# Decoder layer with routed experts: a turn of its own for the last attention chunk, and expert tiles planned from four chunks instead of five

## What is computed

```python
x = x + attn(_layernorm(x))                  # gated linear recurrence over time
x = x + xattn(_layernorm(x), ctx, ctx)       # 16 heads, 77 keys
x = x + ffn(_layernorm(x))                   # 4 experts, each token goes to 2

def ffn(xf):
    scores, idx = top_k(xf @ gate_W + gate_b, 2)
    weights = softmax(scores)
    expert(e) = layernorm(relu(layernorm(xf @ W1[e] + b1[e], g1[e], be1[e])) @ W2[e] + b2[e], g2[e], be2[e])
    return xf + sum over the two chosen experts of weight * expert(e)
```

## Time and profile before

| what | value |
|---|---|
| median of 3 runs | 1317.8 us |
| the profiled execution's own time | 1319.22 us |
| its span | 1317.5 us |
| PE busy | 1205.8 us (92%) |
| DVE busy | 943.1 us (72%) |
| ACT busy | 742.3 us (56%) |
| POOL busy | 435.3 us (33%) |
| chain that ended last | PE 68%, issue 9%, DVE 7%, DMA 5%, ACT 4%, POOL 3% |
| mean granted TensorE clock | 0.949 of full speed |

### The profile page before, as it was taken

One profiled execution on the slowest core, in us unless ns is written; L12 is line 12 of the kernel. 1 busy time (PEld: TensorE's weight loads), 2 busy tenths in 40 slices (PEclk: granted clock), 3 DMA queues, 4 the chain that ended last, 5 costly groups with the idle time before them and its releaser, 6 DMA issues.

```text
span 1317.5 us, 24951 instructions
## 1 busy us (share of the span) xinstructions
PE 1205.8 (92%) x6041; PEld 1004.9 (76%) x6042; DVE 943.1 (72%) x2197; ACT 742.3 (56%) x2119; POOL 435.3 (33%) x392
## 2 busy tenths in 40 slices
PE   5699999999679999999999979689999999999993
PEld 4478888888558888887888867567888888887882
DVE  6688888887635757777678776477777777777772
ACT  4333332233257766577666752276777777777772
POOL 1000000000023313445254434146655545454542
PEclk9789999999879989899899988799999999999996
DMA  9535443343420112022120239754444444444442
GB/s 299 175 128 194 141 158 136 122 156 133 154 82 1 41 57 97 9 93 77 56 96 9 89 119 322 238 161 68 81 80 79 80 79 80 79 80 78 80 66 39
DMA packets 78780, 142.09 MB, mean 108 GB/s; under 512 B 22810, under 2 KB 27086, under 8 KB 76917
## 3 DMA queue, kind: packets, MB, share of 16 engines
q1 hardware_dynamic: 60517, 89.46, 20.6%
q0 software_dynamic: 17056, 35.21, 15.2%
q10 hardware_dynamic: 1152, 16.78, 3.7%
HBM read 77.78 MB, written 66.78 MB: 110 GB/s over the span
## 4 chain that ended last, share of the span: by engine, by line
PE 68%; issue 9%; DVE 7%; DMA 5%; ACT 4%; POOL 3%; SPq 1%; DVEq 1%; POOLq 0%; ACTq 0%
PE banks L960 18%; PE banks L631 18%; PE banks L694 6%; PE banks L814 5%; PE banks L824 5%; PE banks L783 4%; PE banks L800 3%; DMA rows<-slot_table 2%; PE banks L840 2%; ACT rows L1153 2%; DVE operands L1355 2%; PE banks L986 2%; ACT operands L1050 1%; PE banks L972 1%; POOL slot_table L2132 1%
## 5 line engine op out<-in xcount | busy, mean ns | idle before, releaser
L960 PE MATMUL banks<-operands 128*128 x1608 | 390.9, 399 | 29.0 <-ACT banks L1272 13.2
L960 PEld LDWEIGHTS banks<-operands 128*128 128x128 f32 x1608 | 301.4, 190 | 98.9 <-issue 38.6
L631 PE MATMUL banks<-operands 128*128 128x512 f32 (+2 forms) x1224 | 301.1, 404 | 15.4 <-DVE operands L1355 9.4
L631 PEld LDWEIGHTS banks<-operands 128*128 128x128 f32 (+1 forms) x1224 | 233.2, 198 | 65.0 <-DVE operands L1355 8.6
L1355 DVE TENSOR_TENSOR operands<-banks,operands 128x512 fp32r<-128x512 f32 (+3 forms) x328 | 218.4, 682 | 70.1 <-ACT operands L1050 62.8
L1050 ACT ACTIVATE operands<-banks 128x512 fp32r<-128x512 f32 (+3 forms) x328 | 191.4, 603 | 132.2 <-PE banks L814 52.0
L1153 ACT ACTIVATE rows<-banks,score_shift 128x77 f32<-128x77 f32 x512 | 160.4, 361 | 42.2 <-DVE score_shift L1563 40.6
L1050 ACT ACTIVATE operands<-rows 128x512 fp32r<-128x512 f32 (+2 forms) x73 | 54.6, 751 | 173.9 <-DVE rows L1434 135.6
L1284 ACT ACTIVATE banks<-banks,param_cols 128x128 f32<-128x128 f32 x268 | 98.9, 429 | 89.4 <-PE banks L986 89.4
L2119 POOL TENSOR_TENSOR rows<-rows,score_rec 128x1232 f32<-128x1232 f32 x32 | 72.0, 2250 | 170.2 <-DVE score_rec L1571 170.2
L1153 ACT ACTIVATION_READ_ACCUMULATOR rows<-banks,score_shift 128x1 f32 x512 | 124.3, 244 | 0.0
(11 more groups left out here) (174 smaller groups left out, 1668.4 us busy)
## 6 DMA issues: line engine op xcount, KB each, us to landing
expert_parts<-operands SPq DMA_DIRECT2D x32, 512.0 KB, 3.3
operands<-expert_parts ACTq DMA_DIRECT2D x8, 2048.0 KB, 15.1
rows<-in_x SPq DMA_DIRECT2D x8, 1024.0 KB, 5.4
rows<-in_L_ffn_W SPq DMA_DIRECT2D x32, 256.0 KB, 3.7
x_rows<-rows SPq DMA_DIRECT2D x8, 1024.0 KB, 4.4
rows<-x_rows SPq DMA_DIRECT2D x8, 1024.0 KB, 5.8
xf_rows<-rows SPq DMA_DIRECT2D x32, 256.0 KB, 3.2
out<-rows SPq DMA_DIRECT2D x32, 256.0 KB, 2.6
```

Source lines behind the costliest of these rows:

```text
L631: last = nc.tensor.matmul(dst, stationary(a, k), moving(b, k), start=(t == 0 and k == 0), stop=(t == len(terms) - 1 and k == n_k - 1))
L960: last = nc.tensor.matmul(dst, stationary[:, a, k, :], weights[:, bass.ds(e, 1), w, a2, k, :].rearrange("p e f -> p (e f)"), start=False, ...
```

## The change

- `EARLY_CH` falls from 5 to 4, so `EARLY` from 37 to 29; `FRONT` rises from 12 to 18. The early plan moves from DVE's turn 7 into its turn 6 (`planned=True`), the totals from turn 6 to turn 5.
- Every slot load raises one semaphore, with no wait between loads. POOL (for its first gathers), DVE (before its tiles) and ACT (in tile 1) wait for all 29 early loads; after tile 17 all four engines wait for all 67.
- All eight weight loads move to SP; from the second on, each is issued only when the one before has landed. The second waits for the last projection.
- Chunks 6 and 7 get their base rows in place (`base_in_place`), and SP stores them later.
- The last turn gets its own function on each engine; POOL's has both first gathers between `normalise(c, 2)` and `normalise(c, 3)`. Chunk 7's attention output has its own place, and all its projections stand behind the turn.
- In every turn the second `xf_to_features` moves behind `scores(c, 3, (0, 1))`, ACT's third probability piece comes before `exp_scores(c, 2, (3,))`, and DVE's before `invert_sums(c, 2)`.
- Stage C: `weigh`, `slots` and the plan parts move behind `rows_lo` in DVE's tile and spread over tiles 2 to 10; POOL's scatters go one by one over tiles 1 to 12; two waits on slots in each DVE tile and one in each ACT tile go.

The `last_turn` shown in the diff is POOL's; those of PE, ACT and DVE are told above.

```diff
-EARLY_CH = NCH - 3
+EARLY_CH = NCH - 4
 EARLY = 2 * EARLY_CH * TPC - (NE - 1)
-FRONT = 12
+FRONT = 18
...
             engine.wait_ge(plan_ready, 2)
+            engine.wait_ge(slots_in, 16 * NSLOT)
             with engine.Fori(FRONT // 2, (NSLOT - 5) // 2) as n:
...
-            def load_slots(n, u):
-                i = 2 * n + u
+            def load_slots(i):
                 row = sp.value_load(plan_row[0:1, bass.ds(i, 1)], min_val=0, max_val=NE * REG - P)
-                need(sp, slots_in[u], 16 * n)
                 sp.dma_start(tile_slots[:, bass.ds(i, 1), :].rearrange("p i w -> p (i w)"),
-                             slots_d[bass.ds(row, P), :]).then_inc(slots_in[u], 16)
+                             slots_d[bass.ds(row, P), :]).then_inc(slots_in, 16)
...
+            sp.wait_ge(split_out, 16 * 4 * NCH)
             sp.wait_ge(mm_done, mm_num(last - 1, "q3") + 1)
+            load_expert(0)
             load_rows(b1_rows, "L0_ffn_b1", b1_in)
+            sp.wait_ge(plan_ready, 1)
+            sp.wait_ge(scattered, 16 * 2 * TPC * EARLY_CH)
+            with sp.Fori(0, EARLY) as i:
+                load_slots(i)
             for j in range(2):
                 store_xf(last - 1, j)
+            expert_in(0)
...
+            for j in range(TPC):
+                store_base(last - 1, j, slot3(last - 1)[:, j, :])
...
+            sp.wait_ge(mm_done, mm_num(NCH, "o3") + 1)
+            load_expert(1)
             for j in range(TPC):
                 store_xf(last, j)
+            expert_in(1)
+            for s in range(2, 2 * NE):
+                load_expert(s)
                 expert_in(s)
...
             sp.wait_ge(plan_ready, 2)
             sp.wait_ge(scattered, 16 * 2 * (NT - TPC))
             sp.wait_ge(scattered_aside, 16 * 2 * TPC)
-            with sp.Fori(EARLY // 2, NSLOT // 2) as n:
-                load_slot_pair(n)
-            load_slots(NSLOT // 2, 0)
+            with sp.Fori(EARLY, NSLOT) as i:
+                load_slots(i)
...
+            def base_in_place(c, j):
+                act.wait_ge(base_scaled, 2 * c + j // 2 + 1)
+                act.wait_ge(xf_ready, 4 * c + j + 1)
+                nc.scalar.activation(slot3(c)[:, j, :], slot3(c)[:, j, :], ACT.Identity, scale=base_scale[:, j:j + 1],
+                                     bias=base_shift[:, j:j + 1]).then_inc(base_ready, 1)
...
                 if early == 0:
-                    act.wait_ge(mm_done, mm_num(NCH, "o3") + 1)
-                    for s in (5, 6, 7):
-                        load_expert(s)
+                    act.wait_ge(b_t_done, t_num(NCH, "xf3") + 1)
+                    for j in range(TPC):
+                        act.wait_ge(xf_out[j], 16 * NCH)
+                    act.dma_start(be2_rows, io["L0_ffn_be2"].rearrange("e f -> (e f)").partition_broadcast(P).rearrange(
+                        "p (e f) -> p e f", e=NE)).then_inc(be2_in, 16)
...
+            def last_turn(c):
+                normalise(c, 0)
+                scatter(c - 3, 0)
+                scatter(c - 3, 1)
+                normalise(c, 1)
+                ln3_pow(c - 1, 0)
+                scatter(c - 3, 2)
+                scatter(c - 3, 3)
+                normalise(c, 2)
+                for u in range(2):
+                    gather(0, u, own=True)
+                normalise(c, 3)
+                ln3_pow(c - 1, 1)
...
                 if own:
-                    need_alone(pool, slots_in[u], 16 * (n + 1), pool_passed)
+                    need_alone(pool, slots_in, 16 * EARLY, pool_passed)
...
-                if 3 <= early < 7:
-                    scatter(last - 1, early - 3, aside=1)
-                if 8 <= early < 12:
-                    scatter(last, early - 8)
+                if 1 <= early < 5:
+                    scatter(last - 1, 2 + (early - 1) // 2, aside=1, ks=((early - 1) % 2,))
+                if 5 <= early < 13:
+                    scatter(last, (early - 5) // 2, ks=((early - 5) % 2,))
```

More of the change, by code:

```diff
@@ L612, in _ @@
+            for s in range(2, 2 * NE):
+                load_expert(s)
+                expert_in(s)
+            for j in range(TPC):
+                store_base(last, j, slot3(last)[:, j, :])
+            for i in range(2):
+                sp.wait_ge(base_out[i], 16 * 2 * NCH)
+            for j in range(TPC):
+                sp.wait_ge(xf_out[j], 16 * NCH)
             sp.wait_ge(plan_ready, 2)
@@ L926, in b_turn @@
                     gate_scores(c, (2,))
-                if ahead:
-                    scores(c + 1, 1, (0, 1))
+                scores(c + 1, 1, (0, 1))
                 if back:
@@ L948, in _ @@
             b_turn(1, back2=False)
-            with pe.Fori(2, NCH - 2) as c:
+            with pe.Fori(2, EARLY_CH + 1) as c:
                 b_turn(c)
-            b_turn(NCH - 2, totals=True)
-            b_turn(NCH - 1, ahead=False)
+            b_turn(EARLY_CH + 1, totals=True)
+            for c in range(EARLY_CH + 2, NCH - 1):
+                b_turn(c)
             def expert_product(dst, e, w, stationary, ready=None):
@@ L1003, in c_tile @@
                 hidden_in(i, u)
-                if early == 0:
-                    for j in (2, 3):
-                        xf_to_features(last, tail, j)
                 if after >= 3:
@@ L1218, in b_turn @@
                 exp_scores(c, 3, (2,))
[L1219 to L1220 removed]
+                q_hi(c + 1, 1)
                 pT_hi_part(c, 2, (2,))
                 exp_scores(c, 3, (3,))
[L1223 to L1226 removed]
                 if back:
@@ L1835, in b_turn @@
                     ln3_pair(c - 1, 1)
-                if not ahead:
-                    plan_early(0)
                 max_scores(c, 2, 1)
@@ L1841, in b_turn @@
                 pT_lo_part(c, 1, (0, 1))
-                if not ahead:
-                    plan_early(1)
                 if back:
@@ L2025, in c_tile @@
                     rows_lo(i + 3, 1 - u)
+                if early == 2:
+                    weigh(NCH - 1)
+                if early == 3:
+                    slots(NCH - 1, None)
+                if 4 <= early < 9:
+                    plan_late(early - 4)
+                if 9 <= early < 11:
+                    pack_plan(early - 9)
             last, tail = NCH - 1, NCH
-            rows_lo(0, 0)
+            last_turn(last)
             for j in range(2):
@@ L2031, in _ @@
             ln3_pair(last, 0)
+            weigh(last - 1)
+            x2_rows(last, tail, 2)
+            for j in range(2):
+                ln3_apply(last, tail, j)
+            x2_rows(last, tail, 3)
+            ln3_pair(last, 1)
             read_positions(tail)
+            slots(last - 1, tail, aside=1)
+            for j in range(2, TPC):
+                ln3_apply(last, tail, j)
+            rows_lo(1, 1)
             statistics(0, 0, m1_bank[0], m1_done, c1_stat)
```

437 lines of the change are left out of this document (234 added, 203 removed).

## The result

The changed kernel takes 1347.8 us (median of 4 runs, 1346.4 to 1348.7) against 1317.7 us of the kernel before: a ratio of 1.022, with a 95% interval from 1.0189 to 1.025. **It is slower by 30 us, a little over twice the 14 that were forecast**, inside the range only by its last 0.2 us and on the side that had most of the chance. Its profiled execution took 1347.4 us; the span is 1345.5.

What follows compares the result with a forecast made beforehand. PE, busy 92% of the span, was taken as the bound, with slot loads through SP stopping it 28 us at tile 18. Summed, 990.5 - 975.2 - 1.5 = +13.8: 1333.0 profiled, 1332 us median, range 1293 to 1348.

Steps and rivals of the forecast that it cites:

- (a): Order inside turns 1 to 6: 6.5 of 8.4 us of PE's waits for DVE saved, between 3 and 8.4.
- (b): Early plan in turn 6: its small DVE steps delay lo parts PE waits for, costing 1 us (0 to 4).
- (c): Early slots: 29 loads 1.45 us apart; the wait for them puts the last head group at 795.9, before 793.05.
- "free" start: Last head group's start at about 778.6 in the better last-turn order, if it did not wait for the slots.
- (d): Last head group to tile 1: 46 us, before 62.1; tile 1 at 841.9, where it was 855.2.
- (e): Tiles 1 to 12: 2.5 us off 80.1 (between 0 and 6), with tile 12 at 919.5.
- (f): Late slots: 37 distances of 1.45 us, all slots there at 987.6; PE stops 28 us at tile 18.
- first rival: Slot-load loop issues faster without waits, about 0.45 us apart; late slots arrive before tile 18: 1280 us, chance 0.17.
- (g): The 49 tiles behind tile 18: as before, with two waits fewer on DVE, 1.5 us less.
- The fast loop: Slot-load loop without waits runs near the DMA's pace, about 0.45 us apart: 1280 us, chance 0.17.
- The pace of straight line: Rival for the slot loads: the loop runs at straight-line spacing, 1.13 us: 1311, about no change, chance 0.13.
- The third: Rival in tile 0: ACT waits for chunk 7's xf stores behind a weight load, 8 us added: 1340, chance 0.12.

Runs made afterwards that it cites:

- the experiment: Changed kernel with GpSimd's first two gathers behind the last normalise and the rows of tiles 0 and 1 brought in later: 1351.5 us, ratio 1.0232.
- the first profile: Profile of the changed kernel as first measured, with no further edit: 1347.8 us median, ratio 1.022 against the kernel before.
- two steps: Changed kernel with three weights earlier and be2 from SP, 1349.4 us; then also the last two weights issued by ScalarE in tiles 8 and 9, 1351.1 us.
- the second: Profile of the changed kernel measured once more, unedited, on the chip of the experiments: 1351.5 us, ratio 1.0238 against the kernel before.
- the kernel with the two edits: Changed kernel with 24 tiles written out in front instead of 18 and slot loads in straight line: 1306.2 us, ratio 0.9914 against the kernel before.

## Why the prediction was right in kind and wrong in size

**(a), (b) Order of the turns, early plan: near in sum, by errors that cancel.** The six waits of the earlier trace rows are gone from the list over 400 to 753 us; in their place PE waits 2.7 us once for DVE. But from the last `attend` of chunk 0 to that of chunk 5, five turns took 271.6 us before and 254.4 after, 17.2 less, where I had 6.5 for six turns. PE's waits for DVE in them were 7.1 us. The rest is the clock: in three of the five turns before, the mean granted clock is 0.94 (somewhere in each the lower level), and in the five turns after it is 1.00. One such turn before and its like after, columns as in the earlier trace rows:

```profile
483.50:538.40 54.90, 53.85 (x302) 47.33 (x302) 39.37 (x95) 36.02 (x157) 18.14 (x13) 0.94 0.17 59
...
484.00:534.70 50.70, 50.64 (x302) 44.55 (x301) 39.96 (x95) 35.76 (x157) 15.57 (x11) 1.00 0.19 64
```

Against this, turn 6 with the early plan in it took 55.4 us, 4.5 more than the turn before it, where I had 1 (0 to 4), and chunk 0 ended 4.7 us later than before, for a reason that was not looked for. In sum chunk 6's last `attend` ended at 743.0 instead of 752.3, 9.3 us earlier instead of 5.5. The first slot load started at 744.87 us, forecast 746.7.

**(c) Early slots: right.** Spacing 1.49 (1.45), POOL's copy at 788.5 (789), last head group at 794.9 (795.9); the first load was 1.8 us early, which hid the spacing's 28 x 0.04 = 1.1. The "free" start, 778.6, was met by the experiment too: 780.1, with a first load 2.4 us later than in the first profile. What I had not seen is that this stop was no loss to be recovered by itself: taking it away gave nothing, because the first weight's count on SP and POOL's queue come out of the same slot loop. Of the 0.77 us between two loads that I called the row's number going into a register, and set beside the floor of about 600 ns in the Trainium skill's table ("DMA: Bandwidth & Descriptors", latency and other measured facts), the register load itself takes 0.27 us in the profile. The rest is further steps and the gaps between them, so the two figures do not agree; the measured one decides.

**(d) Last head group to tile 1: 52.0 us, not 46.** Tile 1 began at 847.0 instead of 841.9. PE waited 2.2 us for a low part, and tile 0's 24 matmuls ran in part at half clock (0.50 from 838.7 to 843), 7.8 us instead of 5.7 in tile 1, though the forecast had half clock only behind the stop at 794.9. A wait of 1.2 us stands in front of tile 0, whose rstd stood behind four scatter issues on POOL. PE's timeline:

```profile
827.42 3.07 PE L999 MATMUL banks<-operands 128*128 x12 [2.24 <-DVE operands L1405]
...
838.72 7.81 PE L999 MATMUL banks<-operands 128*128 x24
...
848.10 5.71 PE L999 MATMUL banks<-operands 128*128 x24
```

Which of it could be had back was not settled.

**(e) Tiles 1 to 12: the term that failed.** The prediction took 2.5 us off 80.1, with a worst case of nothing gained. Measured were 88.1, 10.5 more than forecast and 8.0 more than before: the term had the wrong sign. I counted DVE's and POOL's instructions and left out the transfers: with weights read one by one, five loads of 2 MB, started from 844.9 to 882.9, are under way in these tiles. The kernel before issued its last three in tile 0, and they had landed at 866.6, when its first scatter-add was issued. Scatter-adds and gathers, which DVE, POOL and PE wait for, land late beside the weights: 9.0 us instead of 4.8 and 6.2 instead of 4.3, as shown above. Taking the weights out in two steps gave 89.5, 84.5, 82.6.

The other part is the place of the extras: behind `rows_lo` they stand in front of the next tile's statistics. With weights earlier, tiles 7 to 11 took 38.3 us with extras behind and 35.9 in front (with 24 tiles in front and straight line beside it), 2.5 us; without, nothing, since the landings took the place. Part of what makes that place dear is a register load: each tile written out begins by reading an expert's number into a register (`expert_at`, L376), and behind the extras, which run one after the other, nothing covers it. VectorE's idle time before the statistics that follow an extra part (total, times, longest), in the changed kernel and in the experiment with the extras in front:

```profile
DVE moe_stats L2020 <- DVE expert_first_tile L1785: 0.8, 1, 0.8
...
DVE moe_stats L2020 <- DVE expert_first_tile L1785: 0.2, 1, 0.2
```

Over the nine places it is 7.8 us against 1.8. Neither part shows alone in the total. The 2.5 us that I took off never came: no experiment has less than 82.0 in these tiles, and the kernel before has 80.1.

The Trainium skill, "DMA: Bandwidth & Descriptors", in its latency table, gives 0.2 us for memory latency on average and 2 us at high load, and says that a DMA's fixed cost grows with it. The late landings agree in direction; the scatter-adds here land 4.2 us later beside the weights, which is more than the 1.8 us between those two figures.

**(f) Late slots: right in mechanism, short by the spacing.** The first late load started 11.6 us behind tile 12 (forecast 12.5), the spacing was 1.54 (1.45: 37 x 0.09 = 3.3 us more), the stop 32.5 us (28). Part of that was a misreading: of the 4.7 us of waits in the earlier trace rows, 1.4 stand at loads before the 31 that I divided by, so the loop without waits costs (49.0 - 3.3) / 30 = 1.52 us, not 1.48. Tile 18 would have been due 1006.4 - 32.5 - 935.1 = 38.8 us behind tile 12; the forecast had 40.0 here, and 38.1 in its first rival, for the same six tiles. The sensitivity of 65 us per us of spacing held: 0.37 us less on average gave 23 us.

**(g) Later tiles: better than forecast.** 285.94 / 44 = 6.50 us a tile against 6.60: 49 x 0.10 = 5 us instead of 1.5. Why is not shown.

The sum, measured less forecast: tile 1 +5.1, tiles 1 to 12 +10.5, start and spacing of the late loads and the start of tile 18 +2.9, half clock behind it -0.6, (g) -3.5: +14.4 on a forecast of 1333.0 is the 1347.4 of the profiled execution.

**The rivals.** The fast loop is out (no loop of loads ran below 1.49 on average in any profile). The pace of straight line was to be had by writing the loop out, at 1.18. The third, ACT waiting for xf stores behind a weight, was there in each profile of that order, but small: 1.3 us in the first, 4.6 in the second, 8.5 when weights came earlier, and 6.0, with a tile 1 of 13.1 us, in the kernel with the two edits. It and the term that failed have the same root; I had placed it at one wait instead of spreading it over the tiles.

By the Trainium skill's rule cited in the prediction ("DMA: Bandwidth & Descriptors", rules for kernel authors), issue early and wait late, the loads should come out at their issue cost. They did, and that was the trouble: the issue cost of 38 loads is 57 us, and the wait was not late enough. Six tiles later the rule held.

## What to carry to other kernels

When many waits, one per use, are merged into one for all, price it as count x issue distance against the time until the first use behind it, and place it behind that point; here 24 tiles written out instead of 18 were worth 34 us. When an order removes short waits that come back in every turn, look at the granted clock beside them: here waits of 7.1 us went, and 17.2 us with them. When a load is moved, list the small transfers that will be under way beside it, and who waits for their landing: it costs there, not where the load is waited for. And before a stop is taken away, look for all that leaves the same queue at the same moment, since the next of them takes its place.

## What the runs showed of the hardware

A register load and a slot load on SP in a loop took 1.49 us on average early in the first profile and 1.50 to 1.61 in the others, for the same instructions; in straight line 1.18 to 1.23. The median hardly moves: 1.48 to 1.52 in every loop of every profile, 1.10 or 1.11 in every straight line. The averages come from a few long distances, up to 3.7 us, whose cause was not looked for. In the views of the loads' lines in the first profile, each load of a row number takes this long (shortest, median, longest in ns):

```profile
L585 SPq TENSOR_LOAD <-plan_rows x67: 262/269/829, 743.8 to 1002.8; - x67
```

The register steps behind it take 0.15, 0.02 and 0.08 us and the DMA 0.35. The loop adds three instructions of 0.05, 0.04 and 0.05 us with their gaps.

On VectorE's sequencer the same kind of load, of an expert's number, stands between the last small step of an extra part and the following statistics, and VectorE sat idle 0.8 to 1.1 us there, at all nine places:

```profile
L376 DVEq TENSOR_LOAD <-plan_experts x9: 301/310/628, 861.5 to 929.6; - x9
...
888.00 0.70 DVE L2020 BATCH_NORM_STATS2 moe_stats<-banks 128x6 f32<-128x512 f32 x1 [0.79 <-DVE expert_first_tile L1785]
```

With the extras in front of the tile's own statistics, the load comes behind `rows_lo`, and the idle time before the statistics is 0.2 us. And the steady tiles, from which the change took two semaphore waits on VectorE and one on ScalarE, and in which it moved `y2` and `be2_rows` to other addresses, became 0.10 us shorter each; which of these did it is not shown.
